# Fetch spread among the small operations of a search, one copy of all turned weights, and a first count moved to ScalarE

## The chip, the core and the metric

The kernel runs on one core of a Trainium2 chip. The metric is device time in microseconds. The change is judged by the median of repeated runs; one further execution, taken by the hardware profiler, gives the page and the trace that are read here. Engines are named as on the page: PE is TensorE, PEld its weight loads, DVE VectorE, ACT ScalarE, POOL GpSimd. L12 is line 12 of the kernel.

## The reference, cut to what matters

Four layers act in order on x of shape (4, 512, 128), each behind a layer norm and added to x: a linear recurrence, a feed-forward layer with FP4 quantisation, the attention, and a mixture of experts. The change touches the attention alone:

```python
dots = einsum('bhid,bhjd->bhij', q, k) * scale          # k: 16 memory keys, then 512
dots = einsum('bhij,hk->bkij', dots, pre_proj)          # heads mixed
dots = where(causal, neg, dots)
vk = top_k(dots, 64)[0][..., -1:]                       # the 64th largest of a row
dots = where(dots < vk, neg, dots)
attn = softmax(dots, axis=-1)
attn = einsum('bhij,hk->bkij', attn, post_proj)
out = einsum('bhij,bhjd->bhid', attn, v)                # then @ Wo + bo
```

There are 4 sequences and 16 heads, so 64 searches for the 64th largest of up to 528 scores in each of 512 rows.

## The kernel before, in words

`g` counts the 64 heads over all sequences. The 512 rows of a head are four tiles of 128 (`t` = 0 to 3), and because of the mask tile `t` has 144, 272, 400 or 528 columns. The head mixing is folded into the projections (`AT`, `Bw`, `G`, `Um`), so a head's scores are one product for each tile. Each engine has its own instruction list, written out by hand as a loop over `g` in which every engine works on several heads at once; semaphores join them. What happens to head `g`:

- PE makes the keys (`keys`, L348) and the scores (`scores`, L363) into the banks `bA` and `bBC`. It is three heads ahead.
- DVE fetches them (`fetch`, L772): one instruction for each tile adds the mask, writes `Sx` in SBUF and the row maximum. `measure` (L783) sums absolute scores in two instructions, as an estimate of a row's spread. It is two heads ahead.
- POOL turns this into a first threshold (`first_threshold`, L1015). The scores above it are counted: tiles 0 to 2 by DVE (`tally`, L792, at the end of its iteration), tile 3 by ACT (`first_tally`, L576) with Sign and an accumulator. `steering` (L1093) writes the constants that turn a count or a sum of signs into the next threshold, by `t < TT - 1`.
- POOL's `second_threshold` (L1025) waits for both counts. ACT counts again (`tally`, L584), POOL corrects (`third_threshold`, L1036), and `shift` (L1045) writes `y`, the scores less the threshold, in four instructions (tiles 3, 2, 1, 0; L1051). ACT counts a third time (`count`, L592).
- DVE's iteration of head `g`: `flip` (L800) forms `away` from two small tensors, `flips`, and turns the signs of `y` into `near`; `nearest` (L811) takes the 8 nearest of each row; `read_hits` (L818) sums on one partition how many rows found their 64th among them, which PE collects (`found`, L408) from POOL's `pick` (`pick_last`, L1053). Then `fetch(g + 2)` and `measure(g + 2)`, then `weights(g)` (L874): three small operations that each need the one before (`picked_top` L877, `vk` L879, `yk` L881), `redo_missed` (L825), which loads a count into a register and branches over a longer search that few heads need, and `keep` (L860), four instructions that read `y` and `Ex`, zero what lies below `yk` and sum the rest; `rinv` (L867) is the reciprocal. Last, `tally(g + 2)`.
- ACT makes the exponentials `Ex` (`weigh`, L600) meanwhile.
- POOL's `spread_scale` (L1063) writes diagonal matrices `spread` from `rinv`, and `mem_w`. PE multiplies the weights by them, which scales and turns them (`turn_weights`, L383): ten 128x128 products into three banks, `bI`, `bG` and `bF`, each with its own semaphore. ACT copies each bank out (`turned_copy`, L610), and PE starts `values` (L392) on the first of the three that is copied. The output of a sequence grows in `bH` over 16 heads.
- After 16 heads, `memory_values` (L413) turns the memory weights in two banks, ACT copies each (`memory_copies`, L624), PE adds their products, and DVE's `take_sum` (L869), at the start of an iteration, takes the result.

The order of one iteration is in the loops at L427 (PE), L630 (ACT), L886 (DVE) and L1077 (POOL):

```python
# PE:   turn_weights(g-1)  found(g)  projected(g)  values(g-1)  scores(g+3)  keys(g+4)  memory_values
# ACT:  key_copy(g+3)  tally(g+1)  turned_copy(g-1) x3  weigh(g+1)  value_copy(g)  count(g+1)  first_tally(g+2)
# DVE:  take_sum  flip(g)  nearest(g)  read_hits(g)  fetch(g+2)  measure(g+2)  weights(g)  tally(g+2)
# POOL: second_threshold(g+1)  pick_last(g)  stage_memory_keys(g+3)  third_threshold(g+1)  shift(g+1)
#       first_threshold(g+2)  spread_scale(g)
```

## Time and profile before

| | |
|---|---|
| median of 3 runs | 1144.14 us (1143.85 to 1145.03) |
| the profiled execution | 1146.44 us, span 1144.7 us |
| mean granted TensorE clock | 0.951 of full speed |
| stretch of the 64 searches | from 247 to 970 us or so |

The span is the time from the first to the last instruction of the profiled execution; a row's times count from its start. A busy time overlaps a little with that of the next instruction, since an instruction's record lasts until its writes are in.

### The profile page before, as it was taken

The numbers are of one execution on the slowest core, as the hardware profiler recorded it, in microseconds if no ns is written. First come the engines' busy times: TensorE is split into PE (matmuls) and PEld (weight loads), VectorE is DVE, ScalarE is ACT, GpSimd is POOL, SyncE is SP. The second block draws the span as 40 slices with busy tenths as digits, with TensorE's granted clock in tenths as the row PEclk, the third lists the DMA queues.
The fourth block names the chain that finished last, engine by engine and source line by source line (L and its number), as shares of the span: only waits on it lengthen the run. The fifth ranks groups of instructions, "written<-read, shape, count | busy, mean of one in ns | idle before, by whom it ended". The sixth has DMA issues, their size and how long they took to land.

```text
span 1144.7 us, 16468 instructions
## 1 busy us (share of the span) xinstructions
PE 952.9 (83%) x4177; PEld 596.3 (52%) x4177; DVE 896.5 (78%) x2990; ACT 709.6 (62%) x1951; POOL 522.5 (46%) x1183
## 2 busy tenths in 40 slices
PE   8759667768888888888889888868988687999998
PEld 4234335436565565656656565545656465633433
DVE  5958687459999998998998999988998987254454
ACT  5032112368888888888888888866888676422221
POOL 5907541036565665655655665644665454000000
PEclk8969889889999999999999999999999998899999
DMA  6000000000000000000000000000000000000000
GB/s 226 1 0 0 1 1 0 1 1 1 1 2 1 2 1 2 1 2 2 1 2 1 1 1 2 1 2 1 2 1 2 1 2 1 1 0 10 9 10 9
DMA packets 5535, 8.82 MB, mean 8 GB/s; under 512 B 1632, under 2 KB 3232, under 8 KB 5280
## 3 DMA queue, kind: packets, MB, share of 16 engines
q1 hardware_dynamic: 5408, 7.51, 2.0%
q14 instruction: 94, 0.77, 0.2%
q8 instruction: 33, 0.54, 0.2%
HBM read 6.46 MB, written 1.05 MB: 7 GB/s over the span
## 4 chain that ended last, share of the span: by engine, by line
DVE 28%; PE 23%; issue 22%; POOL 14%; ACT 6%; POOLq 5%; DVEq 1%; ACTq 0%; DMA 0%
POOL mixed L1051 6%; POOL spread L1070 4%; DVE Ex L864 4%; DVE Sx L780 3%; DVE top L815 2%; DVE mixed L809 2%; PE bA L467 2%; PE bBC L467 2%; DVE unread L796 2%; PE bBC L468 2%; PE bH L486 2%; PE bG L486 2%; PE bI L468 2%; POOL pick L1061 1%; ACT Ex L607 1%
## 5 line engine op out<-in xcount | busy, mean ns | idle before, releaser
L588 ACT ACTIVATE unread<-Sx,nthr 128x144 bf16<-128x144 f32 (+3 forms) x256 | 144.0, 563 | 112.2 <-POOL nthr L1032 112.2
L1051 POOL TENSOR_TENSOR mixed<-Sx,nthr 128x528 f32<-128x528 f32 (+3 forms) x256 | 182.8, 746 | 11.6 <-issue 11.6
L864 DVE SCALAR_TENSOR_TENSOR Ex<-mixed,yk,Ex 128x144 f32<-128x144 f32 (+3 forms) x256 | 130.5, 566 | 46.1 <-DVE yk L881 41.9
L389 PE MATMUL bI<-spread,Ex 128*128 128x128 f32 x384 | 62.6, 302 | 115.7 <-POOL spread L1070 115.7
L1070 POOL TENSOR_TENSOR spread<-ident,rinv 128x512 f32<-128x512 f32 x64 | 66.5, 1039 | 197.6 <-DVE rinv L867 197.6
L596 ACT ACTIVATE unread<-Sx,nthr 128x144 bf16<-128x144 f32 (+3 forms) x256 | 143.7, 571 | 0.0
L389 PEld LDWEIGHTS bI<-spread,Ex 128*128 128x128 f32 x384 | 50.5, 199 | 167.7 <-POOL spread L1070 166.3
L607 ACT ACTIVATE Ex<-Sx,nmax 128x144 f32<-128x144 f32 (+3 forms) x256 | 125.9, 568 | 0.0
L815 DVE MAX8 top<-mixed 128x8 f32<-128x528 f32 (+3 forms) x256 | 110.5, 490 | 0.0
L402 PE MATMUL bH<-turned 128*128 128x512 f32 (+1 forms) x256 | 106.9, 540 | 0.7 <-ACT turned L615 0.7
L809 DVE TENSOR_SCALAR mixed<-mixed,flips 128x528 int32<-128x528 int32 (+3 forms) x256 | 92.1, 419 | 2.5 <-DVE flips L805 0.3
L796 DVE TENSOR_SCALAR_CACHE_REDUCE unread<-Sx,cf 128x144 bf16<-128x144 f32 (+2 forms) x192 | 83.2, 483 | 6.6 <-POOL cf L1021 6.6
L780 DVE CUSTOM_DVE_ANT_0 Sx<-bBC,causal 128x400 f32<-128x400 f32 (+1 forms) x128 | 76.1, 625 | 0.6 <-PE bBC L379 0.6
L360 PE MATMUL bE<-Bw,xn 128*128 128x128 f32 x512 | 75.1, 290 | 0.0
L389 PE MATMUL bF<-spread,Ex 128*128 128x128 f32 x512 | 71.1, 284 | 0.0
L379 PE MATMUL bBC<-Y,xn 128*128 128x512 f32 x128 | 70.7, 634 | 0.0
L360 PEld LDWEIGHTS bE<-Bw,xn 128*128 128x128 f32 x512 | 62.8, 193 | 7.7 <-issue 0.4
L353 PE MATMUL bE<-xn,AT 128*128 128x512 f32 x128 | 65.4, 593 | 0.9 <-DVE xn L717 0.9
L389 PEld LDWEIGHTS bF<-spread,Ex 128*128 128x128 f32 x512 | 66.0, 202 | 0.0
L1000 POOL TENSOR_TENSOR mixed<-wo_s,post_s 128x512 f32<-128x512 f32 x32 | 42.0, 1346 | 48.6 <-PE bH L239 48.6
L376 PE MATMUL bA<-Y,xn 128*128 128x144 f32 (+1 forms) x256 | 56.4, 343 | 2.2 <-issue 1.5
L389 PE MATMUL bG<-spread,Ex 128*128 128x128 f32 x384 | 56.6, 286 | 0.0
(306 smaller groups left out, 2181.2 us busy)
## 6 DMA issues: line engine op xcount, KB each, us to landing
xr<-in_xT SPq DMA_DIRECT2D x4, 256.0 KB, 3.7
w_s<-in_w12T SPq DMA_DIRECT2D x1, 1024.0 KB, 6.4
outT<-xc SPq DMA_DIRECT2D x4, 256.0 KB, 2.0
wq_s<-in_WqT SPq DMA_DIRECT2D x1, 512.0 KB, 3.7
wk_s<-in_WkT SPq DMA_DIRECT2D x1, 512.0 KB, 4.4
wv_s<-in_WvT SPq DMA_DIRECT2D x1, 512.0 KB, 4.0
wo_s<-in_Wo SPq DMA_DIRECT2D x1, 512.0 KB, 4.7
w_s<-in_w3T SPq DMA_DIRECT2D x1, 512.0 KB, 6.6
```

Source lines behind the costliest of these rows:

```text
L360: done = mm(bE[:, jt * P:jt * P + P], xn[:, b, jt * P:jt * P + P], Bw[:, h, :], start=True, stop=True)
L389: last = mm(turn_banks[i][:, k * P:k * P + P], Ex[g % 2][:, t, a:a + P], spread[:, t, :], start=True, stop=True)
L402: last = mm(bH[:, i * P:T], u[:, i, :], PT[i], start=h + i == 0, stop=False)
L588: last = nc.scalar.activation(unread[0][:, OFF[t]:OFF[t] + NT[t]], Sx[g % 2][:, t, 0:NT[t]], ACT.Sign, bias=nthr[g % 2][0][:, t:t + 1], ac ...
L596: last = nc.scalar.activation(unread[2][:, OFF[t]:OFF[t] + NT[t]], Sx[g % 2][:, t, 0:NT[t]], ACT.Sign, bias=nthr[g % 2][1][:, t:t + 1], ac ...
L607: nc.scalar.activation(Ex[g % 2][:, t, 0:NT[t]], Sx[g % 2][:, t, 0:NT[t]], ACT.Exp, bias=nmax[g % 2][:, t:t + 1], scale=1 / DOWN).then_inc ...
L780: V.tensor_tensor_reduce(out=Sx[g % 2][:, t, 0:NT[t]], in0=scores_in[t], in1=causal[:, W - NT[t]:W], scale=DOWN, scalar=LOW, op0=ALU.add, ...
L809: V.tensor_scalar(near[t].bitcast(I32), y[g % 2][t].bitcast(I32), flips[:, t:t + 1], None, ALU.bitwise_xor).then_inc(sem("flipped"), 1)
L815: last = V.max(top[:, t, :], near[t])
L864: V.scalar_tensor_tensor(Ex[g % 2][:, t, 0:NT[t]], y[g % 2][t], yk[:, t:t + 1], Ex[g % 2][:, t, 0:NT[t]], ALU.is_ge, ALU.mult, accum_out=r ...
L1051: Gp.tensor_tensor(y[ph][t], Sx[ph][:, t, 0:NT[t]], nthr[ph][1][:, t:t + 1].broadcast_to((P, NT[t])), ALU.add).then_inc(sem("y_ready"), 1)
L1070: Gp.tensor_tensor(spread[:, :, :], ident[:, :].unsqueeze(1).broadcast_to((P, TT, P)), r[:, :].unsqueeze(2).broadcast_to((P, TT, P)), ALU. ...
```

## The change

Four edits, quoted below in the order of the diff:

- The three tensors `bF`, `bG` and `bI` become parts of one tensor of three banks, `bFGI`. PE writes the ten turned products into it in one row, with one semaphore, `turned_all`; ACT copies all 1280 columns in one instruction; `values` waits for it and runs over `jt` from 0 up.
- The memory weights are likewise turned into one row, copied in one instruction and then multiplied.
- ACT's `first_tally` counts tiles 2 and 3, DVE's `tally` tiles 0 and 1, and `steering` follows.
- `weights(g)` is taken apart. `fetch` now takes the tiles to fetch, and its instructions stand between `picked_top`, `vk` and `yk`; the branch of `redo_missed` stands behind fetch 3, and the second `measure` behind the branch.

```diff
-TURNS = [[(t, 0) for t in range(TT)], [(t, 1) for t in range(1, TT)], [(2, 2), (3, 2), (3, 3)]]
+TURNS = [(t, jt) for jt in range(TT) for t in range(jt, TT)]
...
-bI = pb("bI", 512)
...
-bF = pb("bF", 512)
-bG = pb("bG", 512)
+bFGI = pb("bFGI", 1536)
+bF, bG, bI = (bFGI[:, 512 * i:512 * i + 512] for i in range(3))
...
-quad = [bA[:, :], bBC[:, 0:512], bBC[:, 512:1024], bI[:, :]]
-turn_banks = [bF, bG, bI]
+quad = [bA[:, :], bBC[:, 0:512], bBC[:, 512:1024], bI]
...
-octo = quad + [bE[:, :], bF[:, :], bG[:, :], bH[:, :]]
+octo = quad + [bE[:, :], bF, bG, bH[:, :]]
...
     def turn_weights(g):
...
-        for i in (2, 1, 0):
-            for k, (t, jt) in enumerate(TURNS[i]):
-                a = MEM + jt * P
-                last = mm(turn_banks[i][:, k * P:k * P + P], Ex[g % 2][:, t, a:a + P], spread[:, t, :], start=True, stop=True)
-            last.then_inc(sem(f"turned{i}"), 1)
+        for k, (t, jt) in enumerate(TURNS):
+            a = MEM + jt * P
+            last = mm(bFGI[:, k * P:k * P + P], Ex[g % 2][:, t, a:a + P], spread[:, t, :], start=True, stop=True)
+        last.then_inc(sem("turned_all"), 1)
...
-        for i in (2, 1, 0) if h else (0, 1, 2):
-            pe.wait_ge(sem(f"pt_copied{i}"), g + 1)
-            if i < 2:
-                last = mm(bH[:, i * P:T], u[:, i, :], PT[i], start=h + i == 0, stop=False)
-            else:
-                mm(bH[:, 2 * P:T], u[:, 2, :], PT[2][:, 0:2 * P], start=False, stop=False)
-                last = mm(bH[:, 3 * P:T], u[:, 3, :], PT[2][:, 2 * P:3 * P], start=False, stop=False)
+        pe.wait_ge(sem("pt_copied"), g + 1)
+        at = 0
+        for jt in range(TT):
+            n = T - jt * P
+            last = mm(bH[:, jt * P:T], u[:, jt, :], PT[:, at:at + n], start=h + jt == 0, stop=False)
+            at += n
...
-            bank = turn_banks[1 + i]
...
-                last = nc.tensor.transpose(bank[:, t * P:t * P + P], mem_w[:, t, 8 * i:8 * i + 8, :], ident[:, :])
-            last.then_inc(sem("memT_done"), 1)
+                last = nc.tensor.transpose(bFGI[:, i * T + t * P:i * T + t * P + P], mem_w[:, t, 8 * i:8 * i + 8, :], ident[:, :])
+        last.then_inc(sem("memT_done"), 1)
+        pe.wait_ge(sem("memT_copied"), b + 1)
...
-            pe.wait_ge(sem("memT_copied"), 2 * b + i + 1)
...
     def first_tally(g):
-        t = TT - 1
...
-        nc.scalar.activation(unread[1][:, OFF[t]:OFF[t] + NT[t]], Sx[g % 2][:, t, 0:NT[t]], ACT.Sign, bias=cf[g % 2][:, 0, t:t + 1],
-                             accum_out=above[:, t:t + 1]).then_inc(sem("tallied0_last"), 1)
+        for t in range(2, TT):
+            last = nc.scalar.activation(unread[1][:, OFF[t]:OFF[t] + NT[t]], Sx[g % 2][:, t, 0:NT[t]], ACT.Sign, bias=cf[g % 2][:, 0, t:t + 1],
+                                        accum_out=above[:, t:t + 1])
+        last.then_inc(sem("tallied0_last"), 1)
...
     def weigh(g):
...
-            act.wait_ge(sem("turned0"), g - 1)
+            act.wait_ge(sem("turned_all"), g - 1)
...
-    def turned_copy(g, i):
-        act.wait_ge(sem(f"turned{i}"), g + 1)
+    def turned_copy(g):
+        act.wait_ge(sem("turned_all"), g + 1)
...
-        nc.scalar.activation(PT[i], turn_banks[i][:, 0:P * len(TURNS[i])], cp).then_inc(sem(f"pt_copied{i}"), 1)
+        nc.scalar.activation(PT, bFGI[:, 0:P * len(TURNS)], cp).then_inc(sem("pt_copied"), 1)
...
     def memory_copies(b):
-        for i in range(2):
-            act.wait_ge(sem("memT_done"), 2 * b + i + 1)
-            nc.scalar.activation(memT[:, i, :], turn_banks[1 + i][:, :], cp).then_inc(sem("memT_copied"), 1)
+        act.wait_ge(sem("memT_done"), b + 1)
+        nc.scalar.activation(memT, bFGI[:, 0:2 * T].rearrange("p (i n) -> p i n", i=2), cp).then_inc(sem("memT_copied"), 1)
...
-            for i in (2, 1, 0):
-                turned_copy(g - 1, i)
+            turned_copy(g - 1)
...
     dve.wait_ge(sem("masks_ready"), 1)
-    def fetch(g):
+    def free_for_fetch(g):
         if g >= 2:
             dve.wait_ge(sem("exp_done"), TT * (g - 1))
             dve.wait_ge(sem("counted"), g - 1)
-        for t in range(TT):
+    def fetch(g, tiles):
+        for t in tiles:
             if t != 1:
                 dve.wait_ge(sem("s_done"), 3 * g + (1, 0, 2, 3)[t])
             V.tensor_tensor_reduce(out=Sx[g % 2][:, t, 0:NT[t]], in0=scores_in[t], in1=causal[:, W - NT[t]:W], scale=DOWN, scalar=LOW,
                                    op0=ALU.add, op1=ALU.max, accum_out=rmax[g % 2][:, t:t + 1]).then_inc(sem("fetched"), 1)
-    def measure(g):
-        x = Sx[g % 2]
+    def measure_first(g):
         dve.wait_ge(sem("fetched"), TT * g + 1)
-        V.tensor_reduce(size[g % 2][:, 0:1], x[:, 0, MEM:MEM + SAMPLE[0]], AX.X, ALU.add, apply_absolute_value=True)
+        V.tensor_reduce(size[g % 2][:, 0:1], Sx[g % 2][:, 0, MEM:MEM + SAMPLE[0]], AX.X, ALU.add, apply_absolute_value=True)
+    def measure_others(g):
         dve.wait_ge(sem("fetched"), TT * g + 4)
-        V.tensor_reduce(size[g % 2][:, 1:TT], x[:, 1:TT, MEM:MEM + SAMPLE[1]], AX.X, ALU.add,
+        V.tensor_reduce(size[g % 2][:, 1:TT], Sx[g % 2][:, 1:TT, MEM:MEM + SAMPLE[1]], AX.X, ALU.add,
                         apply_absolute_value=True).then_inc(sem("sized"), 1)
     def tally(g):
         dve.wait_ge(sem("thr0_ready"), g + 1)
-        for t in range(TT - 1):
+        for t in range(2):
             last = V.tensor_scalar(unread[1][:, OFF[t]:OFF[t] + NT[t]], Sx[g % 2][:, t, 0:NT[t]], cf[g % 2][:, 0, t:t + 1], 0.0, ALU.is_ge, ALU.add,
                                    accum_out=above[:, t:t + 1])
         last.then_inc(sem("tallied0"), 1)
...
         dve.wait_ge(sem("att_done"), b + 1)
         V.scalar_tensor_tensor(xr[:, b, :], bH[:, :], vecs[:, 4:5], xr[:, b, :], ALU.add, ALU.add).then_inc(sem("sum_taken"), 1)
-    def weights(g):
+    def pick_tops(g):
         dve.wait_ge(sem("topped"), 2 * g + 2)
         V.tensor_tensor(picked_top[:, :, :], pick[:, :, 0:WIN], top[:, :, :], ALU.mult).then_inc(sem("top_picked"), 1)
+    def add_tops(g):
         dve.wait_ge(sem("top_picked"), g + 1)
         V.tensor_reduce(vk[:, :], picked_top[:, :, :], AX.X, ALU.add).then_inc(sem("vk_ready"), 1)
+    def last_kept(g):
         dve.wait_ge(sem("vk_ready"), g + 1)
         V.tensor_tensor(yk[:, :].bitcast(I32), vk[:, :].bitcast(I32), flips[:, :], ALU.bitwise_xor).then_inc(sem("yk_ready"), 1)
-        redo_missed(g)
-        dve.wait_ge(sem("yk_ready"), g + 1)
-        keep(g)
     for g in range(-2, HEADS):
+        there, coming = 0 <= g, g + 2 < HEADS
         if g > H and g % H == 1:
             take_sum(g // H - 1)
-        if 0 <= g:
+        if there:
             flip(g)
             nearest(g, (3, 2))
             nearest(g, (1, 0))
             read_hits(g)
-        if g + 2 < HEADS:
-            fetch(g + 2)
-            measure(g + 2)
-        if 0 <= g:
-            weights(g)
-        if g + 2 < HEADS:
+        if coming:
+            free_for_fetch(g + 2)
+            fetch(g + 2, (0,))
+        if there:
+            pick_tops(g)
+        if coming:
+            fetch(g + 2, (1,))
+        if there:
+            add_tops(g)
+        if coming:
+            fetch(g + 2, (2,))
+        if there:
+            last_kept(g)
+        if coming:
+            measure_first(g + 2)
+            fetch(g + 2, (3,))
+        if there:
+            dve.wait_ge(sem("yk_ready"), g + 1)
+            redo_missed(g)
+        if coming:
+            measure_others(g + 2)
+        if there:
+            dve.wait_ge(sem("yk_ready"), g + 1)
+            keep(g)
+        if coming:
             tally(g + 2)
     centre(3, range(B - 1))
     take_sum(B - 1)
...
-            pool.wait_ge(sem("turned0"), g)
+            pool.wait_ge(sem("turned_all"), g)
...
-            pool.wait_ge(sem("memT_done"), 2 * b)
+            pool.wait_ge(sem("memT_done"), b)
...
-    if t < TT - 1:
+    if t < 2:
...
```

## Rows read from the trace of the kernel before

**Rows 1.** The page's busy time of each engine, share of the span, instructions.
```profile
PE 952.9 (83%) x4177; PEld 596.3 (52%) x4177; DVE 896.5 (78%) x2990; ACT 709.6 (62%) x1951; POOL 522.5 (46%) x1183
```

**Rows 2.** Busy time of each engine in the stretch of one head.
```profile
635.48:646.28 10.80, 9.30 (x50) 6.60 (x50) 10.08 (x41) 9.34 (x27) 6.61 (x18) 1.00 0.01 2
```

**Rows 3.** Who waited for whom, 250 to 980 us: total, times, longest.
```profile
DVE Ex L864 <- DVE yk L881: 41.9, 59, 0.9
```

**Rows 4.** VectorE's groups by form, 250 to 950 us: busy, mean ns, idle before.
```profile
L872 DVE SCALAR_TENSOR_TENSOR xr<-bH,vecs,xr 128x512 f32<-128x512 f32 x3 | 2.3, 750 | 2.6 <-PE bH L423 2.6
...
L831 DVE MATCH_REPLACE8 mixed<-top,mixed 128x528 f32<-128x528 f32 x3 | 2.1, 693 | 0.0
```

**Rows 5.** Timeline of one head: start, duration, instruction, idle before.
```profile
634.16 0.18 DVE L867 RECIPROCAL rinv<-rsum 128x4 f32<-128x4 f32 x1
...
634.42 1.04 POOL L1070 TENSOR_TENSOR spread<-ident,rinv 128x512 f32<-128x512 f32 x1 [2.61 <-DVE rinv L867]
...
635.48 0.25 DVE L803 TENSOR_TENSOR away<-over,steer_s 128x4 f32<-128x4 f32 x1
...
635.52 0.94 PE L389 MATMUL bI<-spread,Ex 128*128 128x128 f32 x6 [1.50 <-POOL spread L1070]
...
635.67 0.20 POOL L1030 TENSOR_TENSOR moved<-above,cf 128x4 f32<-128x4 f32 x1
...
636.25 0.41 ACT L588 ACTIVATE unread<-Sx,nthr 128x144 bf16<-128x144 f32 x1 [1.46 <-POOL nthr L1032]
...
637.49 0.38 POOL L1061 TENSOR_SCALAR pick<-pick 128x64 f32<-128x64 f32 x1 [0.16 <-issue]
...
638.41 0.19 ACT L588 ACTIVATION_READ_ACCUMULATOR unread<-Sx,nthr 128x1 f32 x1
...
638.50 0.47 ACT L615 ACTIVATE turned<-bI 128x384 f32<-128x384 f32 x1
...
639.14 0.64 PE L404 MATMUL bH<-turned 128*128 128x256 f32 x2
...
639.21 0.28 DVE L780 CUSTOM_DVE_ANT_0 Sx<-bA,causal 128x144 f32<-128x144 f32 x1
...
639.24 0.58 ACT L615 ACTIVATE turned<-bF 128x512 f32<-128x512 f32 x1
...
639.39 2.86 POOL L1051 TENSOR_TENSOR mixed<-Sx,nthr 128x528 f32<-128x528 f32 x4 [0.18 <-issue]
...
640.92 0.18 DVE L787 TENSOR_REDUCE size<-Sx 128x1 f32<-128x48 f32 x1
...
641.03 0.55 DVE L789 TENSOR_REDUCE size<-Sx 128x3 f32<-128x384 f32 x1
...
641.49 0.43 DVE L877 TENSOR_TENSOR picked_top<-pick,top 128x32 f32<-128x32 f32 x1
...
642.88 0.37 DVE L864 SCALAR_TENSOR_TENSOR Ex<-mixed,yk,Ex 128x144 f32<-128x144 f32 x1 [0.54 <-DVE yk L881]
...
643.80 1.02 PE L353 MATMUL bE<-xn,AT 128*128 128x512 f32 x2
...
644.29 0.73 ACT L581 ACTIVATE unread<-Sx,cf 128x528 bf16<-128x528 f32 x1
...
644.96 0.18 DVE L867 RECIPROCAL rinv<-rsum 128x4 f32<-128x4 f32 x1
...
645.73 0.62 DVE L796 TENSOR_SCALAR_CACHE_REDUCE unread<-Sx,cf 128x400 bf16<-128x400 f32 x1
```

**Rows 6.** Timeline of single GpSimd and VectorE instructions.
```profile
641.23 0.64 POOL L1051 TENSOR_TENSOR mixed<-Sx,nthr 128x272 f32<-128x272 f32 x1
...
959.98 1.04 POOL L1070 TENSOR_TENSOR spread<-ident,rinv 128x512 f32<-128x512 f32 x1 [2.67 <-DVE rinv L867]
...
960.30 0.73 DVE L803 TENSOR_TENSOR away<-over,steer_s 128x4 f32<-128x4 f32 x1 [0.40 <-ACT unread L596]
```

**Rows 7.** GpSimd's groups by form, 250 to 950 us.
```profile
L1051 POOL TENSOR_TENSOR mixed<-Sx,nthr 128x528 f32<-128x528 f32 x62 | 66.1, 1066 | 11.3 <-issue 11.3
```

More of the change, by code:

```diff
@@ L119, in mixed_layers_kernel @@
         U_st = [turned[:, 3 + i, :].rearrange("p (t d) -> p t d", t=TT) for i in range(2)]
-        PT = [turned[:, i, 0:P * len(TURNS[i])] for i in range(3)]
+        PT = turned[:, 0:3, :].rearrange("p i n -> p (i n)")[:, 0:P * len(TURNS)]
         mem_w = sb("mem_w", [P, TT, H, MEM])
```

## Prediction

> **What bounds the kernel now.** I read the busy shares first [rows 1]: VectorE is busy 78% of the span, TensorE 83%, ScalarE 62%. TensorE's share is the larger, but it is an average over all stages, so I went on to the stretch of one head [rows 2]: a head of the search takes 10.80 us and VectorE is busy for 10.08 of them. The waits [rows 3] then say who is waited for: VectorE's only regular wait is on itself, 41.9 us in 59 heads (0.71 each) between `yk` (L881) and the first `keep` (L864), while ScalarE, TensorE and GpSimd wait for things that VectorE releases. In the code that wait is the load of `hits` into a register and the branch on it (L829). So VectorE's own order sets the pace, and in the head laid out on the clock [rows 5] the only idle time in front of one of its instructions is the 0.54 us at L864.
>
> An ordinary head takes 10.80 us with a wait of 0.54; at the mean wait of 0.71 it takes 10.97. There are 64 heads (4 sequences of 16), so 63 intervals. Three hold `take_sum` and three a repeated search (one widest L831 for each) [rows 4]; one interval is both, and I set aside the two behind the other repeats, which leaves 56 ordinary ones.
>
> **The changes, on the clock of one head.** I count from the start of `rinv` (634.16) to the next (644.96) [rows 5] and give each event as time after it. Before: POOL's `spread` 0.26 to 1.30, VectorE's `away` (L803) 1.32 to 1.57, POOL's second threshold from 1.51, which lets ScalarE's tally start at 2.09; that ends at 4.44, the three copies run from 4.34, POOL's four `y` instructions (L1051) from 5.23 to 8.09, VectorE's fetch from 5.05, the small operations from 7.33, `keep` from 8.72, `rinv` again at 10.80.
>
> *First count of tile 2 moved.* VectorE loses one instruction of 400 columns: from its start (645.73) to `away` (646.28) that is 0.55 us. ScalarE gains one: it takes 0.73 us for 528 columns (L581), and 128 columns cost 0.11 (0.58 less 0.47, L615), so 400 cost some 0.62. But VectorE doesn't get the 0.55. `away` reads two SBUF operands, and the trace shows such instructions wait out the GpSimd instruction that is under way [rows 5, 6]: L803 at 960.30 took 0.73 us instead of 0.25 and ended at 961.03, just when `spread` (959.98, 1.04) ended at 961.02; L877 at 641.49 took 0.43, to 641.92, beside a `y` instruction that ended at 641.87. With a shorter tally `away` comes at 0.77, in the middle of `spread`, and ends at 1.32 instead of 1.57. The gain is 0.24, not 0.55. All that follows on VectorE moves by this: fetch 0 at 4.81.
>
> *Small operations between the fetches.* Today L877, L879 and L881 take 641.49 to 642.88, 1.39 us, less the wait 0.85 (half of it the collision just described). In the new order L877 comes at 5.03, 0.20 before POOL's first `y` instruction at 5.23, so it should find GpSimd idle. Each small operation, no longer waiting for the one in front, then costs about what L787 costs (0.11, from 640.92 to 641.03). The bounds of the three together are 0.33 and today's 0.85. The four fetches take 1.71 (639.21 to 640.92), which I share by columns with 0.08 for each start. So: L877 at 5.03, fetch 1 at 5.14 (0.36), L879 5.50, fetch 2 5.61 (0.50), L881 6.11. This one reads two SBUF tensors as well (`vk`, `flips`), and POOL's first `y` instruction is under way until 6.30, so it is through at 6.33 by the same collision. Then the first measure 6.33 (0.11), fetch 3 6.44 (0.63), the second measure 7.07 (0.46, from 641.03 to 641.49), ready for `keep` at 7.53 instead of 8.72.
>
> *The load and branch.* They now stand behind fetch 3. Bounds: all of the 0.71 goes (the sequencer works while fetch 3 runs, 0.63) or nothing does (it starts when fetch 3 is through; then `keep` is ready at 8.24). I take the first: while fetch 3 runs nothing that the load needs is open. The next paragraph brings the two ends close to each other. No row of this trace tells how far the sequencer runs ahead. The Trainium skill, Perfetto Trace Analysis, "DVE / Act Engine Instruction", has the sequencer free for the next instruction as soon as one is pushed to the wait queue; by it the whole wait would be hidden, and the sum would be the same, for the reason that follows.
>
> *What is late next.* `keep` reads two SBUF operands (`y` and `Ex`) and would start at 7.53, while POOL's `y` instructions run until 8.09, as their start hangs on the chain `rinv`, `spread`, `nthr`, ScalarE tally, `nthr` again, none of which the change shortens. Before, `keep` came at 8.72, clear of them. The first ends at 6.30 (1.07 long) [rows 7], the third at 7.71 [rows 6], the last at 8.09 [rows 5]. So `keep` of tile 0 waits until 7.71 and runs some 0.3; the last `y` instruction, behind it, goes to some 8.45; the other three `keep`s and the step to `rinv` take the rest of today's 2.08, 1.78: 10.23. If `keep` waits for all four `y` instructions instead, it is 8.15 + 2.08 = 10.23 as well. If `keep` shared the access freely, it would be 7.53 + 2.08 = 9.61; that is the lower bound, and 10.80 with no gain the upper; I go by the L803 of rows 6, the nearest case. If the branch is not covered, `keep` starts at 8.24, clear of POOL, and the head takes 10.32. **Forecast: 10.25 us a head.** The bound is no longer VectorE's own sum (9.6) but the loop from `rinv` over POOL and ScalarE to `y` and back.
>
> *The other engines at 10.25.* ScalarE: from the tally's start to the end of the first count (636.25 to 645.02) 8.77; less 0.09 for two copies fewer (384 columns take 0.37 from start to start, of which 0.33 is columns by the 0.11 above, so some 0.04 is fixed); plus 0.62; plus 0.77 from there to the next tally (0.19 for the accumulator's read, 0.58 from L1030 to the tally's start): 10.07. It fits, by 0.2. The bounds of the single copy over three banks, which the trace doesn't show: 1.12 us by that slope, 1.52 by the sum of the three durations (0.47, 0.47, 0.58); I take 1.15, nearest to the slope of the same instruction. TensorE: `values` began at 639.14, behind the first copy; now it begins behind the only one, at 639.8, 0.65 later. Its keys then end at 645.5, which is 11.3; the next turn can start at 10.25 + 1.36 = 11.6. So the lost overlap costs nothing as long as the slack of 0.3 is there; at 1.52 for the copy the excess of 0.4 would eat ScalarE's slack and cost 0.2 a head. The search for the hits is unhurt: `pick` ends at 3.71 (637.49 and 0.38), and the hits are read at about 4.6. POOL's waits for `turned_all` and `memT_done` ask for events that are 6 us old.
>
> *Sum.* 56 ordinary heads by 0.72 (10.97 less 10.25): 40. `take_sum` waits for the memory products; TensorE comes to them 1.2 us later, ScalarE ends its longer first count before the copy, and the copy isn't overlapped: 0 to 2.5 each, I take 1.2 net in three, 3.5. The last head's copy and memory product stand free: 0.65 and 0.5. The first heads pay the longer first count once: 0.6. Repeats: no change. Together some 5.5 back, 35 gained. Of the profiled execution's 1146.44 us remain 1111.5; the median of the runs is 2.3 below that execution, so 1109.
>
> **The rivals**, each with the median it gives. (a) *The shared access costs less than I think, and ScalarE bounds*: 10.07 a head; 56 by 0.90 less 5.5: 45 gained, 1099. For it: none of the collisions in rows 5 and 6 shows `keep`. Against: it has the same two operands. Chance 0.10.
>
> (b) *The load and branch cost more where they stand now*: VectorE may have to drain before the load, and the branch empties what was queued behind it, so the second measure and the first `keep` both come late. From the bound above, 8.24, and one more half of the 0.71 (the measure restarting an empty queue): 8.6 and 2.08, 10.68 a head; 56 by 0.29 less 5.5: 11 gained, 1133. For it: today's 0.54 to 0.9 idle us there [rows 3, 5] are just this. 
> (c) *L877 falls behind the first `y` instruction, and the kernel is slower.* My margin is 0.20 us: it is lost once L877 starts after 5.23. Then L877 ends with that instruction at 6.30, fetch 1 runs 6.35 to 6.71, L879 to 6.82, fetch 2 to 7.32, L881 waits for the third `y` instruction until 7.71, measure, fetch 3 and measure follow, and `keep` is ready at 8.95: 11.03 a head. 56 by 0.06 lost and 5.5 more: 1153. For it: one small wait more in front is enough, and each of the three small operations now stands inside POOL's stretch, where before only L877 did. Against: both starts hang on the same `rinv`, so they move together. The Trainium skill, SBUF — State Buffer, "SBUF: two separate sides", has the rule: a VectorE instruction with two SBUF inputs and a GpSimd one that reads SBUF exclude each other for a whole instruction. The collisions in rows 5 and 6 agree. Chance 0.13.
>
> (d) *Nothing comes of it*: the time moves by under 0.2% (2.3 us), because TensorE, out of its overlap, takes the pace with about 10.9. That needs 0.8 us more than the chain above gives it. Chance 0.04.
>
> **How the numbers follow.** The forecast has 0.55; 0.05 is left for other ways, 0.04 of them gains. What a measurement of this kernel can tell from no change is about 0.2%. Faster: 0.55, 0.10, 0.14 and 0.04 make 0.83; within 0.2%: 0.03 and 0.01; slower: 0.13. The range goes from (a) to beyond (b), 1097 to 1138, and takes in the unknown ends: 0.2 a head for the copy (11 us), 2.5 for each `take_sum`. It leaves out (c).
>
> **What would show it.** Head to head at 10.2 to 10.3; L803 near 0.55 us long and ending with `spread`; L877 under 0.2 long; the first L864 longer than its 0.37 by 0.1 to 0.5, beside an L1051; ScalarE's wait for `nthr` (L588) down from 1.46 to about 0.3 to 0.5; TensorE waiting for the copy at `values`. The step on the branch is right if the idle time in front of L789 is under 0.3, wrong from 0.6 (then (b)). I am wrong if L864 runs at 0.37 beside an L1051 (then (a)), if L877 takes over 0.8 (c), or if TensorE has no idle time left in a head.

## The result, and the profile after

| | before | after |
|---|---|---|
| median of 3 runs | 1144.14 us | 1110.47 us (1106.15 to 1111.49) |
| after / before | | 0.9694, 95% interval [0.9668, 0.9719] |
| span of the profiled execution | 1144.7 us | 1108.8 us |
| mean of the 56 ordinary heads (the 56 shortest of the 63 intervals from `rinv` to `rinv`) | 10.93 us | 10.19 us |

The change saves 33.7 us; 35 were forecast.

The seven intervals set aside are the seven longest of each kernel, and that is not quite the prediction's rule. Its count "one interval is both" is wrong: with heads counted from 0, `take_sum` stands in the intervals that end with heads 17, 33 and 49, and the repeated searches in those that end with heads 46, 48 and 58, so that with the two behind the repeats (47 and 59) there are eight. The 55 intervals that are left at the same places in both kernels have means of 10.92 and 10.17, so the difference stays 0.74 to 0.75.

The lines that moved: `fetch` is L777, `measure` L783 and L788, `tally` L795, `away` L802, `keep` L863, `rinv` L866, `take_sum` L871, `picked_top` L876, `vk` L881, `yk` L886; on ScalarE `first_tally` L576, `tally` L584, the turned copy L611, the memory copy L623; on GpSimd the second threshold L1052 and L1054, `y` L1073, `spread` L1092; on TensorE the turned products L386, `values` L400, the memory products L414 and L418.

The page's busy times (us, share of the span, instructions), where VectorE has lost 9 us and ScalarE has gained 36 [rows 1]:

```profile
PE 958.9 (86%) x4177; PEld 595.4 (54%) x4177; DVE 887.2 (80%) x2862; ACT 746.1 (67%) x1947; POOL 554.5 (50%) x1183
```

The stretch of one head, laid out as in [rows 2]: the window, its length, the busy time of TensorE, its weight loads, VectorE, ScalarE and GpSimd (instructions in brackets), the granted clock, the DMA share and GB/s. ScalarE is now busy for 9.96 of 10.26 us, against 9.34 of 10.80:

```profile
640.75:651.01 10.26, 9.32 (x51) 6.63 (x50) 10.12 (x39) 9.96 (x28) 7.46 (x17) 1.00 0.01 2
```

The same head on the clock, to be laid beside [rows 5]:

```profile
640.75 0.18 DVE L866 RECIPROCAL rinv<-rsum 128x4 f32<-128x4 f32 x1
...
641.01 1.04 POOL L1092 TENSOR_TENSOR spread<-ident,rinv 128x512 f32<-128x512 f32 x1 [0.91 <-DVE rinv L866]
...
641.52 0.55 DVE L802 TENSOR_TENSOR away<-over,steer_s 128x4 f32<-128x4 f32 x1
641.59 0.73 ACT L576 ACTIVATE unread<-Sx,cf 128x528 bf16<-128x528 f32 x1
...
642.55 0.36 POOL L1052 TENSOR_TENSOR moved<-above,cf 128x4 f32<-128x4 f32 x1 [0.25 <-ACT unread L576]
...
643.30 0.41 ACT L584 ACTIVATE unread<-Sx,nthr 128x144 bf16<-128x144 f32 x1 [0.30 <-POOL nthr L1054]
...
645.54 1.22 ACT L611 ACTIVATE turned<-bFGI 128x1280 f32<-128x1280 f32 x1
...
645.69 0.17 DVE L876 TENSOR_TENSOR picked_top<-pick,top 128x32 f32<-128x32 f32 x1
...
646.45 2.97 POOL L1073 TENSOR_TENSOR mixed<-Sx,nthr 128x528 f32<-128x528 f32 x4 [0.18 <-issue]
...
646.74 0.80 DVE L886 TENSOR_TENSOR yk<-vk,flips 128x4 int32<-128x4 int32 x1
...
646.90 2.39 PE L400 MATMUL bH<-turned 128*128 128x512 f32 x8 [0.63 <-ACT turned L611]
...
648.31 0.55 DVE L788 TENSOR_REDUCE size<-Sx 128x3 f32<-128x384 f32 x1
...
648.78 0.36 DVE L863 SCALAR_TENSOR_TENSOR Ex<-mixed,yk,Ex 128x144 f32<-128x144 f32 x1
...
649.06 0.66 DVE L863 SCALAR_TENSOR_TENSOR Ex<-mixed,yk,Ex 128x272 f32<-128x272 f32 x1
...
651.01 0.18 DVE L866 RECIPROCAL rinv<-rsum 128x4 f32<-128x4 f32 x1
```

No VectorE row of the head has idle time in front of it, and yet VectorE is waiting: `yk`, four numbers a row, lasts 0.80 us and ends at 647.54, when GpSimd's first `y` instruction (646.45, 1.07 long) ends at 647.52. Such waits are inside the durations. The groups by form of 250 to 920 us show how much of them there is (busy, mean ns, idle before):

```profile
L886 DVE TENSOR_TENSOR yk<-vk,flips 128x4 int32<-128x4 int32 x63 | 35.7, 567 | 0.0
...
L863 DVE SCALAR_TENSOR_TENSOR Ex<-mixed,yk,Ex 128x272 f32<-128x272 f32 x63 | 34.9, 553 | 0.0
...
L788 DVE TENSOR_REDUCE size<-Sx 128x3 f32<-128x384 f32 x62 | 34.3, 553 | 9.2 <-DVE rmax L777 6.1 <-issue 2.2
...
L802 DVE TENSOR_TENSOR away<-over,steer_s 128x4 f32<-128x4 f32 x63 | 33.5, 532 | 0.6 <-ACT unread L592 0.6
...
L863 DVE SCALAR_TENSOR_TENSOR Ex<-mixed,yk,Ex 128x144 f32<-128x144 f32 x63 | 28.2, 448 | 1.0 <-ACT Ex L603 1.0
...
L876 DVE TENSOR_TENSOR picked_top<-pick,top 128x32 f32<-128x32 f32 x63 | 13.9, 220 | 0.0
```

In the kernel before these took 168 (`yk`), 498, 544 (`measure`), 246 (`away`), 369 and 403 ns. So `picked_top` waits 0.18 us less a head, `yk` 0.40 more, `away` 0.29 more, the first two `keep`s together 0.13 more; the idle time of [rows 3] is gone. The waits of 250 to 940 us (total, times, longest) have `nthr` down to 19.5 us, from 111.9 (250 to 980 us there), and new ones for the single copies:

```profile
PE bH L400 <- ACT turned L611: 36.3, 57, 1.4
...
ACT unread L584 <- POOL nthr L1054: 19.5, 32, 1.8
...
DVE xr L871 <- PE bH L418: 12.8, 3, 4.8
...
PE bH L418 <- ACT turned L623: 7.2, 4, 3.9
```

**The balance.** I cut the span at the `rinv` rows: up to the first, the 56 ordinary intervals, the 7 others (sequence ends, repeated searches and what follows them), from the last `rinv` to the last `take_sum`, and from there to the end. Saved, in us: 1.8 (257.5 to 255.6), 41.3 (56 by 0.74), then lost 2.1 (99.5 to 101.6), 3.0 (9.86 to 12.90) and 2.0 (166.0 to 168.0): 36.0, the difference of the spans. The first and the last of these parts are not the change's doing, as shown under "The ends" below.

### The profile page after: what moved, and what is told of

Its sections match the earlier page's. It is cut to its first block, busy times and chain, and to the rows that moved or that the text cites. A ratio compares the mean times of both kernels' runs of the same rounds, so it can differ in the third digit from the quotient of the medians.

```text
span 1108.8 us, 16210 instructions
## 1 busy us (share of the span) xinstructions
PE 958.9 (86%) x4177; PEld 595.4 (54%) x4177; DVE 887.2 (80%) x2862; ACT 746.1 (67%) x1947; POOL 554.5 (50%) x1183
## 4 chain that ended last, share of the span: by engine, by line
DVE 53%; PE 25%; issue 10%; ACT 7%; POOL 2%; DVEq 1%; POOLq 1%; ACTq 1%; DMA 0%
DVE Ex L863 11%; DVE top L814 7%; DVE mixed L808 6%; DVE Sx L777 4%; DVE unread L795 3%; DVE yk L886 2%; PE bA L462 2%; PE bBC L462 2%; DVE away L802 2%; PE bBC L463 2%; PE bH L481 2%; PE bFGI L481 2%; PE bFGI L463 2%; PE bFGI L386 2%; ACT unread L584 1%
## 5 line engine op out<-in xcount | busy, mean ns | idle before, releaser
L1073 POOL TENSOR_TENSOR mixed<-Sx,nthr 128x528 f32<-128x528 f32 (+3 forms) x256 | 185.5, 757 | 11.6 <-issue 11.6
L386 PEld LDWEIGHTS bFGI<-spread,Ex 128*128 128x128 f32 x1280 | 155.1, 199 | 65.4 <-POOL spread L1092 63.3
L400 PE MATMUL bH<-turned 128*128 128x512 f32 (+3 forms) x512 | 153.1, 442 | 36.6 <-ACT turned L611 36.3
L386 PE MATMUL bFGI<-spread,Ex 128*128 128x128 f32 x1280 | 164.9, 286 | 22.1 <-POOL spread L1092 22.0
L584 ACT ACTIVATE unread<-Sx,nthr 128x144 bf16<-128x144 f32 (+3 forms) x256 | 144.0, 564 | 23.8 <-POOL nthr L1054 19.8
L400 PEld LDWEIGHTS bH<-turned 128*128 128x128 f32 x512 | 92.0, 189 | 97.0 <-issue 76.7
L863 DVE SCALAR_TENSOR_TENSOR Ex<-mixed,yk,Ex 128x144 f32<-128x144 f32 (+3 forms) x256 | 139.1, 596 | 1.7 <-ACT Ex L603 1.0
L1092 POOL TENSOR_TENSOR spread<-ident,rinv 128x512 f32<-128x512 f32 x64 | 66.6, 1041 | 87.5 <-DVE rinv L866 87.5
L576 ACT ACTIVATE unread<-Sx,cf 128x400 bf16<-128x400 f32 (+1 forms) x128 | 85.6, 673 | 10.6 <-POOL cf L1043 10.6
L611 ACT ACTIVATE turned<-bFGI 128x1280 f32<-128x1280 f32 x64 | 77.9, 1218 | 14.6 <-PE bFGI L386 14.6
L808 DVE TENSOR_SCALAR mixed<-mixed,flips 128x528 int32<-128x528 int32 (+3 forms) x256 | 84.4, 391 | 2.5 <-DVE flips L804 0.2
L777 DVE CUSTOM_DVE_ANT_0 Sx<-bBC,causal 128x400 f32<-128x400 f32 (+1 forms) x128 | 79.7, 623 | 0.6 <-PE bBC L377 0.5
L374 PE MATMUL bBC<-Y,xn 128*128 128x400 f32 x128 | 54.0, 504 | 0.3
## 6 DMA issues: line engine op xcount, KB each, us to landing
xr<-in_xT SPq DMA_DIRECT2D x4, 256.0 KB, 3.6
outT<-xc SPq DMA_DIRECT2D x4, 256.0 KB, 2.0
```

What stands on the lines that cost most here:

```text
L374: last = mm(scores_in[t], x_t, k[:, 0:NT[t]], start=True, stop=True)
L386: last = mm(bFGI[:, k * P:k * P + P], Ex[g % 2][:, t, a:a + P], spread[:, t, :], start=True, stop=True)
L400: last = mm(bH[:, jt * P:T], u[:, jt, :], PT[:, at:at + n], start=h + jt == 0, stop=False)
L584: last = nc.scalar.activation(unread[0][:, OFF[t]:OFF[t] + NT[t]], Sx[g % 2][:, t, 0:NT[t]], ACT.Sign, bias=nthr[g % 2][0][:, t:t + 1], ac ...
L777: V.tensor_tensor_reduce(out=Sx[g % 2][:, t, 0:NT[t]], in0=scores_in[t], in1=causal[:, W - NT[t]:W], scale=DOWN, scalar=LOW, op0=ALU.add, ...
L808: V.tensor_scalar(near[t].bitcast(I32), y[g % 2][t].bitcast(I32), flips[:, t:t + 1], None, ALU.bitwise_xor).then_inc(sem("flipped"), 1)
```

## The experiments

Each was timed in five rounds beside the kernel before, which had medians of 1144.8 to 1146.1 us. A head is the mean of the 56 shortest `rinv` to `rinv` intervals of its trace. One trace is one execution, and the part behind the searches alone, where all kernels do the same, lasts from 165.0 to 169.1 us in them, so a difference of a few us between two medians is read together with the parts of the span.

**The order alone.** The kernel before with the taken-apart `weights` and `fetch` of the change, and nothing else.

> The kernel before with the new order of VectorE's list alone (fetches among the small operations, branch behind fetch 3). With the count of tile 2 still on VectorE, away ends at 1.57 after rinv as before, so L877 comes at 5.27, just behind the start of POOL's first y instruction at 5.23. Theory 'shared access' (a VectorE instruction with two SBUF inputs waits out a GpSimd instruction): L877 lasts about 1.0 us, yk waits again, and a head takes about 11.0: 1145 to 1152 us, no gain at all. Rival 'order only' (what counts is the wait for the load and branch, 0.71, and 0.4 of small operations): 9.9 to 10.1 a head, about 1095 us.

Measured: 1147.17 us, ratio 1.0012 [0.9994, 1.0031], a head 11.00. No gain at all. Its group by form, and one head's GpSimd and VectorE rows:

```profile
L882 DVE TENSOR_TENSOR picked_top<-pick,top 128x32 f32<-128x32 f32 x58 | 55.9, 963 | 0.0
```

```profile
637.27 2.86 POOL L1079 TENSOR_TENSOR mixed<-Sx,nthr 128x528 f32<-128x528 f32 x4 [0.18 <-issue]
...
637.31 1.07 DVE L882 TENSOR_TENSOR picked_top<-pick,top 128x32 f32<-128x32 f32 x1
```

`picked_top` comes 0.04 us behind the start of `y` and stays until the first `y` instruction is through. This is rival (c) as it was written, 11.03 us a head.

**The same instructions, `picked_top` first.** To take the collision away and leave the rest, `picked_top` goes in front of fetch 0, some 0.2 us earlier.

```diff
-if coming: free_for_fetch(g + 2); fetch(g + 2, (0,))
 if there:  pick_tops(g)
+if coming: free_for_fetch(g + 2); fetch(g + 2, (0,))
```

> The kernel before with the new order alone, as in the run 'reorder alone' (10.996 a head, 1147 us, L877 0.96 us long because it came at 5.27 after rinv and POOL's first y instruction had started at 5.23), but with L877 in front of fetch 0 instead of behind it, so 0.22 us earlier, at 5.05. Nothing else differs, not one instruction. Theory 'shared access': L877 now finds GpSimd idle and lasts about 0.2; yk still waits for the first y instruction; a head takes 10.2 to 10.35, about 1108 us (and less for the ends of the sequences, which keep three and two copies: down to 1102). Rival 'the order of the small operations is worth what it is worth, GpSimd aside': as before, 1147.

Measured: 1117.15 us, 0.9759 [0.9736, 0.9783], a head 10.39. Thirty us from one place in the list, though 9 less than was expected: `yk` was to wait for the first `y` instruction only. In its trace `picked_top` is through as `y` starts, and `yk` is now the one that is held. It starts just behind the end of the first `y` instruction and stays until the second ends. That is so where `y` starts at 5.23 to 5.26 (34 of the 55 heads at common places, mean 10.49); where it starts later, `yk` meets the first only (mean 10.23):

```profile
639.85 0.17 DVE L882 TENSOR_TENSOR picked_top<-pick,top 128x32 f32<-128x32 f32 x1
640.04 2.86 POOL L1078 TENSOR_TENSOR mixed<-Sx,nthr 128x528 f32<-128x528 f32 x4 [0.18 <-issue]
...
641.12 0.81 DVE L892 TENSOR_TENSOR yk<-vk,flips 128x4 int32<-128x4 int32 x1
```

**The count alone.** The kernel before with ACT's `first_tally` over tiles 2 and 3.

```diff
-        t = TT - 1
+        for t in range(2, TT):
...
-        for t in range(TT - 1):
+        for t in range(2):
...
-            if t < TT - 1:
+            if t < 2:
```

> The kernel before with the first count of tile 2 on ScalarE alone. Theory 'shared access': VectorE gives up 0.55 but away then waits for spread (away lasts about 0.55), so a head gains 0.24: 10.69, about 1131 us. Rival 'VectorE's sum': it gains the whole 0.55, about 1114 us. ScalarE's own order (10.16 with three copies) bounds in neither.

Measured: 1120.53 us, 0.978 [0.9761, 0.9799], a head 10.50: 0.43 less. Neither theory gave that (10.69, or the whole 0.55). `away` lasts 530 ns, so 0.28 of the 0.55 goes into the wait for `spread`, as the prediction has it. But the rest of the head moved against `y` as well: `picked_top` takes 288 ns instead of 403, and the wait in front of `keep` is 33.1 us in 57 heads (0.58) instead of 41.9 in 59, while `yk` takes 297 instead of 168. The prediction's 0.24 misses what comes of that.

**The copies alone.** The kernel before with `bFGI`, one turned copy and one memory copy (its main lines).

```diff
-            for i in (2, 1, 0):
-                turned_copy(g - 1, i)
+            turned_copy(g - 1)
```

> The kernel before with one copy of the turned weights and one of the memory weights alone. TensorE waits some 0.65 longer for the copy in each head, but has 1.5 idle, so an ordinary head stays at 10.93. What it costs stands at the end of each sequence, where the memory products come later: 1 to 2.7 us for each of four. Expected 1148 to 1154. Rival 'fewer instructions help': ScalarE saves 0.09 a head, which is worth nothing while VectorE bounds, so 1144 or below would speak for it.

Measured: 1153.29 us, 1.0069 [1.0053, 1.0085]: 8 us longer, and clear of noise. A head stays at 10.92, as nobody waits for ScalarE there. Of the 7.5 us by which its span is longer, 5.4 stand up to the last `take_sum`, and at the ends of sequences: 2.8 between the last `rinv` and `take_sum` (9.86 to 12.65), and two intervals with `take_sum` grow by 1.6 each (12.78 to 14.39). The last 2.0 come behind `take_sum`, where the two kernels do the same.

**The change with three copies.** The order and the count, with the copies as before (main lines).

```diff
-            turned_copy(g - 1)
+            for i in (2, 1, 0):
+                turned_copy(g - 1, i)
```

> The changed kernel with the three copies and the two memory copies as before. Ordinary heads: by 'ScalarE's order bounds' (its own sum is 10.07 and its idle time in the changed kernel 0.3 to 0.4 a head) 0.09 more, 10.28 instead of 10.19, 5 us lost; by 'the loop from rinv over y to keep bounds' unchanged. Ends of sequences: the 2.7 us in three heads and 3 at the end come back, 11 us gained. So 1104 by the first, 1099 by the second. If the single copy were worth having, it would be above 1110.

Measured: 1109.43 us, 0.9687 [0.967, 0.9704]. Within the interval of the whole change, and above both values expected (1104 and 1099). In a head the single copy earns 0.12 (10.31 to 10.19), 6.6 us over 56, a little more than the 0.09 of 'ScalarE's order bounds'. The ends give 5.4 of it back, 2.7 in the seven other intervals and 2.7 from the last `rinv` to `take_sum` (10.16, against 12.90), where 11 had been expected. So here the two single copies together are worth some 1 us.

**The memory copies in two.** The whole change, and only the memory weights copied bank by bank again, in `bFGI`.

```diff
-        act.wait_ge(sem("memT_done"), b + 1)
-        nc.scalar.activation(memT, bFGI[:, 0:2 * T] ...)
+        for i in range(2):
+            act.wait_ge(sem("memT_done"), 2 * b + i + 1)
+            nc.scalar.activation(memT[:, i, :], bFGI[:, i * T:i * T + T], cp) ...
```

> The changed kernel with two memory copies, each with its own semaphore, as before; the turned weights are still copied at once. Ordinary heads unchanged at 10.19. The end of a sequence took 14.8 us with one copy of both and 13.5 with three and two copies. The first product can start after a copy of 0.6 instead of 1.02 and the second copy runs beside it: 0.5 to 0.9 less at each of four ends, 2 to 4 us: about 1107. If the longer way at the ends comes from the late start of TensorE alone, no gain: 1110.

Measured: 1102.42 us, 0.9624 [0.9605, 0.9644], 8 less than the whole change, where 3 were expected. Of 8.1 us of span, 4.4 come in the 63 intervals (3.6 of it in the three with `take_sum`), 1.1 between the last `rinv` and `take_sum`, and 3.0 behind it. The 3.0 are not the edit's: behind `take_sum` both kernels do the same. What is left for the two memory copies is about 5.

**ScalarE 0.3 us shorter.** The value copy of a head copies only the first 128 of its 512 columns; the kernel leaves the rest out, so that its attention output is not the reference's.

```diff
-nc.scalar.activation(U_st[g % 2], bE[:, :] ...)
+nc.scalar.activation(U_st[g % 2][:, 0, :], bE[:, 0:P], cp) ...
```

> The changed kernel in which ScalarE's copy of the projected values (L618) takes 128 of its 512 columns; the other three tiles' values are not copied, so the attention output is not the reference's, and the search is untouched. It takes 0.32 us a head from ScalarE and nothing from any other engine. Theory 'ScalarE's order bounds': a head falls by 0.2 to 0.32, to 9.9 or 10.0, 1093 to 1100 us. Theory 'the loop from rinv over y to keep bounds', in which the tally waits for spread and VectorE: 10.1 to 10.2, 1106 to 1111.

Measured: 1100.09 us, 0.9602 [0.9583, 0.9621], a head 10.04, between the two theories. ScalarE gets 0.32 us and the head 0.15. Head by head the reason is plain. In the whole change `y` starts either 5.36 us after `rinv` (34 heads) or 5.7 (22 heads; in 20 of them GpSimd's L1052 had waited 0.25 us for ScalarE's first count); `yk` then takes 0.46 or 0.80. Here `y` is late in 2 heads (the same 2 in which no such wait is seen in the whole change), and `yk` takes 444 ns instead of 567. With three copies it is late in 49, and the head takes 10.31.

**`yk` before fetch 2.**

```diff
-fetch(g + 2, (2,))
 last_kept(g)
+fetch(g + 2, (2,))
```

> The changed kernel with yk moved one place forward, in front of fetch 2, so that it comes before POOL's y instructions. In the changed kernel yk lasts 0.57 us in the mean, 0.4 of it waiting for GpSimd. Theory 'VectorE's list bounds, waits for the shared access counted in': a head falls from 10.19 to about 9.8, 1088 us. Theory 'ScalarE's order bounds' (10.07 of its own and what POOL adds between the first count and the next tally): 10.1 to 10.2, 1106 to 1111 us, and the time freed turns up as longer keeps or another wait on VectorE.

Measured: 1114.8 us, 0.973 [0.9711, 0.9748], a head 10.22: no gain, and the median is 4 us above the whole change and outside both ranges expected. (The trace is of its fastest execution, 1108.17 us.) `yk` starts 0.4 us earlier and takes 729 ns instead of 567: it ends with the same `y` instruction, and fetch 2, which used to fill that time, now comes behind it. `keep` then comes clear of `y` (395 ns instead of 448 for its first).

**The branch back behind the second measure.**

```diff
-redo_missed(g)
 measure_others(g + 2)
+redo_missed(g)
```

> The changed kernel with the load and branch where they were, behind the second measure and directly in front of keep. If hiding them behind fetch 3 is worth its 0.71: VectorE has no idle time in the changed kernel, so a head rises by 0.71 less what the keeps then no longer wait for GpSimd (0.2): 10.7, about 1138 us. If ScalarE's order bounds with VectorE only just under it, the rise is smaller, 0.3 to 0.4: about 1130. If the place of the branch doesn't matter: 1110.

Measured: 1111.21 us, 0.9694 [0.9675, 0.9714], a head 10.26. The idle time in front of the first `keep` (L863, timeline) is a third of what it was:

```profile
641.90 0.55 DVE L788 TENSOR_REDUCE size<-Sx 128x3 f32<-128x384 f32 x1
642.64 0.42 DVE L863 SCALAR_TENSOR_TENSOR Ex<-mixed,yk,Ex 128x144 f32<-128x144 f32 x1 [0.19 <-issue]
```

The time is that of the last of the three cases expected: the place hardly matters. Over all heads the idle time is 23.8 us in 62 (0.38), against 0.71 behind the short `yk`. So the load and branch need not stand early; an instruction of half a us in front hides about half of them. The head is 0.07 longer in the mean: 0.13 of the idle time is paid for by `keep`'s wait for `y`, which no longer occurs (390 and 495 ns), and `y` is late in 2 heads instead of 22, as ScalarE has more time. Between heads in which `y` is not late it is 10.27 against 10.07.

**`take_sum` later.** On the kernel with `picked_top` first, and on the changed one with two memory copies, `take_sum` goes behind `read_hits`.

The lines below are shortened.

```diff
-if g > H and g % H == 1: take_sum(g // H - 1)
 if there: flip(g); nearest(...); read_hits(g)
+if g > H and g % H == 1: take_sum(g // H - 1)
```

> The kernel of the run 'reorder, picked_top first' with take_sum behind read_hits instead of at the start of the iteration. VectorE no longer waits for the memory products with its whole list behind; they are done by then. The head with take_sum, 12.8 with it in front, falls by its excess of 1.9 less 0.67 for the operation itself, unless TensorE, which turns the next head's weights only behind the memory products, gives the hits late: then 0.5 to 1.2 less. 2 to 4 us in all for three heads. If TensorE's own order sets these heads, nothing.

> The changed kernel with two memory copies (1102.4 us in the run before) and take_sum behind read_hits. Heads with take_sum took 13.9 to 14.1. TensorE ended the turned weights of the next head 3 us after the memory products and then found the hits; VectorE would read them at once instead of 1.2 us later: 0.5 to 1.2 less a head, 1099 to 1101. If TensorE's own order sets these heads, nothing: 1102.

Measured: 1114.42 us, 0.9742 [0.9721, 0.9763], against 1117.15 without; and 1099.22 us, 0.9598 [0.9585, 0.9611], against 1102.42. VectorE's wait for the memory products leaves the sequence ends in both. In the first pair two intervals of 13.50 become 11.91 and the third goes from 13.01 to 12.72, while an ordinary head is 0.07 longer (10.46), as `y` is late in fewer of them; in the second, 13.89 and 14.07 become 12.75 and 12.93, but the third grows from 11.92 to 12.35. Each pair's intervals of the ratio overlap, so neither gain is clear of noise. The last kernel has the lowest median of those that compute the whole: 45 us below the kernel before, 11 below the change.

## Why the prediction was right

**The bound and the forecast of a head: right.** 10.25 was forecast, 10.19 measured, and by the mechanism named: VectorE's list is short enough, and what it waits for is inside its two-operand instructions beside GpSimd. That the two numbers are so close is partly luck, as two errors below cancel. The Trainium skill, SBUF — State Buffer, "SBUF: two separate sides", calls it an exclusive lock for the whole of an instruction; `picked_top` at 1.07 in one list and 0.17 in another, moved by 0.2 us, agrees.

**The count: `away` right, the total too small.** `away` was to be near 0.55 and is 532 ns, ending with `spread` (642.07 and 642.05). The count by itself brought 0.43, not 0.24.

**The small operations: right, with one term off.** `picked_top` was to start at 5.03 after `rinv` and last under 0.2: it starts at 4.94 and lasts 0.17. `yk` was to be held until 6.33; it is held until 6.44 in the heads where `y` starts at 5.36, and until 6.79 in the 22 others. The term that is off is the start of `y`, kept at 5.23 because the change shortens nothing of its chain. The change lengthens it, in two ways. In nearly every head it is 0.12 later, and the run with the count alone shows the same (5.35). There `near` starts 0.2 earlier, and GpSimd's instruction of four numbers that starts beside it, at 1.85 in both, takes 0.31 instead of 0.20. Before, and with the count alone (each head's own `rinv` is at 634.16 and 471.08):

```profile
635.97 1.45 DVE L809 TENSOR_SCALAR mixed<-mixed,flips 128x528 int32<-128x528 int32 x4
636.01 0.20 POOL L1032 TENSOR_TENSOR nthr<-moved,cf 128x4 f32<-128x4 f32 x1
```

```profile
472.69 1.31 DVE L810 TENSOR_SCALAR mixed<-mixed,flips 128x528 int32<-128x528 int32 x4
472.93 0.31 POOL L1033 TENSOR_TENSOR nthr<-moved,cf 128x4 f32<-128x4 f32 x1
```

And in 20 heads ScalarE's longer first count makes it 0.35 later still. The short value copy takes that second delay away and earns 0.15 a head.

**The branch: right.** The idle time in front of L788 is 9.2 us in 62 (0.15), under the 0.3 asked for. The run with the branch moved back adds that its early place is worth 0.07 a head and not more.

**`keep`: right in kind, smaller.** It was to be longer by 0.1 to 0.5; its first two are longer by 0.08 and 0.06, and 0.2 where it meets the end of a `y` instruction. In the forecast `keep` was ready at 7.53 and lost 0.62 to `y` from there on (10.23 less 9.61). Over the 55 intervals at common places it starts at 7.93, and from its start to `rinv` it is 2.24, only 0.16 more than the 2.08 of before. So what stands in front of `keep` took 0.40 more than forecast, above all because `yk` was held longer, and the wait in `keep` 0.46 less: these are the two errors that cancel.

**ScalarE and TensorE: right, but ScalarE's slack was too large.** 10.07 was worked out for ScalarE, 0.2 under the head. In 27 of the 56 heads its idle time is only 0.14 us, in front of L584, and they average 10.10. In the head shown above there is no slack: it is busy for 9.96 and waits 0.30 for a threshold that had itself waited for its first count, and the two make the 10.26 of the head. The short term was the way from the end of that count (642.32) to the next tally (643.30): 0.98, where 0.77 was counted, as L1052 takes 0.36 there and not 0.20. The single copy takes 1.22 (1.15 forecast), its wait for `nthr` is 0.30 in most heads that have one, and TensorE waits 0.64 for the copy without harm.

**The ends: right in sum, by luck.** 5.5 us were to be given back, 5.4 were (41.3 less 36.0). But the start gained 1.8 where 0.6 was to be lost, and 2.0 were lost behind the last `take_sum`, which the sum did not have. Both follow TensorE's granted clock. Its mean up to the first `rinv` is 0.861 before and 0.867 after, 35.8 and 34.1 us short of full speed, a difference of 1.7. Over the 13 traces the first `rinv` comes at 256.8 to 258.2 us where that mean is 0.861, at 255.1 to 256.0 where it is 0.867, and at 253.5 to 254.5 where it is 0.873. Two kernels that differ only behind it (`take_sum` later or not) stand in two of these groups, 255.2 and 253.8, and each group holds kernels with and without the moved count. The last section has the same for the stretch behind `take_sum`. So neither part is the change's, and they cancel here by chance.

The last head was put at 1.15, and the time from the last `rinv` to `take_sum` grew by 3.0. In the kernel before (timeline, TensorE and ScalarE):

```profile
971.06 0.83 PE L389 MATMUL bI<-spread,Ex 128*128 128x128 f32 x6
...
972.52 0.47 ACT L615 ACTIVATE turned<-bI 128x384 f32<-128x384 f32 x1
...
973.29 0.60 PE L404 MATMUL bH<-turned 128*128 128x256 f32 x2
...
976.74 1.98 PE L423 MATMUL bH<-turned,Um 128*128 128x512 f32 x4 [0.25 <-ACT turned L628]
...
978.76 0.75 DVE L872 SCALAR_TENSOR_TENSOR xr<-bH,vecs,xr 128x512 f32<-128x512 f32 x1 [6.81 <-PE bH L423]
```

and in the one after:

```profile
930.56 2.39 PE L386 MATMUL bFGI<-spread,Ex 128*128 128x128 f32 x20
...
932.99 1.24 ACT L611 ACTIVATE turned<-bFGI 128x1280 f32<-128x1280 f32 x1 [0.88 <-PE bFGI L386]
...
934.38 2.39 PE L400 MATMUL bH<-turned 128*128 128x512 f32 x8 [1.42 <-ACT turned L611]
...
937.68 1.02 ACT L623 ACTIVATE turned<-bFGI 128x1024 f32<-128x1024 f32 x1 [3.45 <-PE bFGI L414]
938.76 1.98 PE L418 MATMUL bH<-turned,Um 128*128 128x512 f32 x4 [1.11 <-ACT turned L623]
940.78 0.75 DVE L871 SCALAR_TENSOR_TENSOR xr<-bH,vecs,xr 128x512 f32<-128x512 f32 x1 [9.33 <-PE bH L418]
```

From the first turned product to `values` it is 2.23 before and 3.82 after: not only the copy is longer (the 0.65 forecast), it also starts when all ten products are out instead of the first three, 0.97 later. From `values` to the memory products it is 3.45 and 4.38, 0.9 where 0.5 was forecast. The remaining 0.5 is TensorE's layer norm products in front of the turned ones: they start 0.5 later against `rinv`. What was called 1.15 is a mis-sized term, 2.5.

**The rivals.** (a), ScalarE alone at 10.07: with 0.32 us less on ScalarE the head would then have come to 9.75, and it came to 10.04, so ScalarE is not the only bound: of the 0.32 only 0.15 came through. (b) is refuted by the idle time at L788. (c) was real: it is the order alone, and it happened once inside the change, in an ordinary head where `y` started at 5.24 instead of 5.36 and `picked_top` at 5.28. That head took 11.04 us. VectorE had been idle for 0.23 us in front of `near` (its first row here), which put `picked_top` 0.34 later; why it was idle no run shows:

```profile
800.70 1.45 DVE L808 TENSOR_SCALAR mixed<-mixed,flips 128x528 int32<-128x528 int32 x4 [0.23 <-DVE flips L804]
...
804.13 2.86 POOL L1073 TENSOR_TENSOR mixed<-Sx,nthr 128x528 f32<-128x528 f32 x4 [0.18 <-issue]
804.17 1.07 DVE L876 TENSOR_TENSOR picked_top<-pick,top 128x32 f32<-128x32 f32 x1
```

What keeps the others out of it is the moved count: it brings `picked_top` 0.3 us forward. The prediction gave the margin (0.20) and did not say that the count made it. Its chances also differ in one place: (d) has 0.04 in its paragraph and 0.03 in the sum.

## What to carry to other kernels

Look inside the durations, not only at the idle time: a small two-operand VectorE instruction that lasts five times its usual length is a wait for GpSimd, and its place in the list, a few tenths earlier or later, can be worth more than the instructions around it. An edit that gains nothing alone may gain beside another, which moves it out of a collision: the new order alone gained nothing (1147 us), the count alone 24 us (1121), and both, with the copies as before, 36 (1109), so the order was worth 11 us once the count had moved. And a transfer joined from several into one saves a little in the steady state (0.12 us a head here, and only where ScalarE is nearly the bound) and pays at each end of the pipeline, where nothing overlaps it: keep the joined form in the loop, the split one at the ends. Last, before two variants a few us apart are compared, look whether the difference stands where they differ.
